# A routed-experts kernel: half rows and scatters for the late tiles, against whole rows and two tiles summed by 0/1 products

## The reference

```python
x = x + _L0_ffn_ref(_L0_cond_ref(x, cond_128, ...), L0_ffn_w_gate, L0_ffn_w_up, L0_ffn_w_down)
x = x + _L1_ffn_ref(_L1_cond_ref(x, cond_128, ...), L1_ffn_gate_w, L1_ffn_expert_w, L1_ffn_expert_b)

# _L1_ffn_ref: 32 experts, each token goes to its best two
logits = xf @ gate_w.T
w, idx = jax.lax.top_k(logits, 2)
w = jax.nn.softmax(w, axis=-1)
combine = zeros((T, 32)).at[arange(T)[:, None], idx].add(w)
out = sum over experts e of combine[:, e, None] * (xf @ expert_w[e].T + expert_b[e])
```

## Time and profile before

| | us |
|---|---|
| median of 3 runs | 294.91 |
| profiled execution | 294.77 |
| its span, first to last instruction | 292.9 |
| PE busy, share of the span | 261.6, 89% |
| DVE, ACT, POOL busy | 130.5, 77.4, 76.3 |
| bytes read from and written to HBM | 50.70 MB, 10.32 MB |

### The profile page before, as it was taken

How to read it: one execution, slowest core, us unless ns; L and a number is a source line. 1 busy time by engine, 2 the same in 40 slices (tenths; PEclk the granted TensorE clock), 3 DMA queues, 4 the chain that set the end, 5 groups by cost and what they waited for, 6 DMA issues and landing times.

```text
span 292.9 us, 4645 instructions
## 1 busy us (share of the span) xinstructions
PE 261.6 (89%) x1672; PEld 163.0 (56%) x1672; DVE 130.5 (45%) x386; ACT 77.4 (26%) x142; POOL 76.3 (26%) x77
## 2 busy tenths in 40 slices
PE   7877999999999999999999999999999999995000
PEld 3345677688777778788877764323333335662000
DVE  3368666767613335567313364105744112200374
ACT  2556665244011133333301112111011112121000
POOL 1522400000000000017150224576444542455000
PEclk9999999999999999999999999999999999999555
DMA  7990000000000100073049998259999999941896
GB/s 274 398 337 3 3 0 0 3 0 2 0 36 36 38 37 0 2 281 151 1 174 396 418 417 341 68 152 378 400 420 416 405 414 418 412 195 50 282 366 211
DMA packets 21671, 58.13 MB, mean 198 GB/s; under 512 B 4569, under 2 KB 12417, under 8 KB 17296
## 3 DMA queue, kind: packets, MB, share of 16 engines
q1 hardware_dynamic: 15216, 46.84, 41.2%
q0 software_dynamic: 3968, 8.43, 7.9%
q10 hardware_dynamic: 2464, 2.56, 2.5%
HBM read 50.70 MB, written 10.32 MB: 208 GB/s over the span
## 4 chain that ended last, share of the span: by engine, by line
PE 84%; DMA 7%; SPq 3%; DVE 2%; ACT 2%; issue 1%; ACTq 0%; POOLq 0%
PE bank L1338 27%; PE bank L1484 25%; PE bank L1520 14%; PE bank L1456 4%; DMA wbuf<-r_tab 4%; PE bank L1393 3%; DMA xp_first<-in_xp 2%; PE bank L1221 2%; PE bank L1414 2%; SPq L593 2%; PE bank L1400 1%; DMA r_tab<-res,row_halves 1%; PE bank L1283 1%; DVE y0lo L899 1%; PE bank L1231 1%
## 5 line engine op out<-in xcount | busy, mean ns | idle before, releaser
L1484 PE MATMUL bank<-wbuf,xT 128*32 128x512 f32 (+3 forms) x560 | 77.9, 512 | 0.0
L1520 PE MATMUL bank<-md,hid 128*128 128x512 f32 x176 | 48.2, 414 | 0.0
L623 POOL DMA_INDIRECT slots<-kept,sid x16 | 15.9, 994 | 122.1 <-DVE sid L1005 119.1
L1484 PEld LDWEIGHTS bank<-wbuf,xT 128*64 128x64 f32 (+1 forms) x560 | 27.9, 124 | 34.9 <-issue 27.6
L1520 PEld LDWEIGHTS bank<-md,hid 128*128 128x128 f32 x176 | 31.7, 189 | 8.3 <-issue 2.9
L1338 PE MATMUL bank<-y0hi,mg 128*128 128x512 f32 x88 | 35.2, 411 | 0.6 <-ACT y0hi L709 0.6
L1041 DVE COPY xT<-bank 128x512 f32<-128x512 f32 x21 | 14.5, 691 | 46.1 <-PE bank L1456 46.0
L827 ACT ACTIVATE res<-bank,recs 128x512 f32<-128x512 f32 (+1 forms) x27 | 16.0, 593 | 71.5 <-PE bank L1484 71.5
L1338 PE MATMUL bank<-y0hi,mu 128*128 128x512 f32 x88 | 33.7, 396 | 0.7 <-DVE mu L903 0.7
L1338 PE MATMUL bank<-y0lo,mg 128*128 128x512 f32 x88 | 33.7, 394 | 0.2 <-DVE y0lo L899 0.2
L1338 PE MATMUL bank<-y0lo,mu 128*128 128x512 f32 x88 | 33.6, 393 | 0.0
(11 more groups left out here) (187 smaller groups left out, 273.6 us busy)
## 6 DMA issues: line engine op xcount, KB each, us to landing
wbuf<-in_w SPq DMA_DIRECT2D x32, 1024.0 KB, 12.0
wbuf<-r_tab SPq DMA_DIRECT2D x8, 512.0 KB, 8.8
acc<-in_x SPq DMA_DIRECT2D x1, 2048.0 KB, 15.3
y_tab<-yv SPq DMA_DIRECT2D x8, 256.0 KB, 4.2
out<-acc ACTq DMA_DIRECT2D x8, 256.0 KB, 5.0
base<-in_base SPq DMA_DIRECT2D x3, 352.0 KB, 7.0
xp_first<-in_xp SPq DMA_DIRECT2D x1, 1040.0 KB, 6.9
xp_second<-in_xp SPq DMA_DIRECT2D x1, 1040.0 KB, 9.1
```

What stands on the lines that cost most here:

```text
L623: pool.indirect_dma_start(out=slots, out_offset=bass.IndirectOffsetOnAxis(ap=sid[:, j, k:k + 1], axis=0), in_=rec[:, j, k], in_offset=None ...
L1484: v = mm(in_place(RS[n % 2], h)[p0:p0 + w], xT[x_slot(t)][:, c, p0:p0 + w], wbuf[buffer(r)][:, c, columns(h)], start=(c == 0), stop=(c == ...
L1520: v = mm(DN[j % 2][:], hid[:, t, part, c], md[:, c], start=(c == 0 and part == 0), stop=(c == HC - 1 and part == 1))
```

## The change

- The steps in halves are gone. All 21 tiles are whole rows, with two places of `xT`. A scatter is 2 KB for each row.
- Only tiles 0 to 18 are scattered (TD = 19). The rows of tiles 19 and 20 stay in SBUF: ACT writes the scaled rows, rounded to float32r, to `rows{i}0`, and DVE computes the rest, scale times bank minus rounded, to `rows{i}1` (`low_part`). For each of the two tiles DVE builds a matrix `hot[i]` of 0 and 1, 128 rows by 1024 tokens (`one_hot`, from a new word 3 of the records). PE multiplies it with the rows for each block j of 128 tokens (`add_up`): two tiles, two parts, 8 blocks, 32 products of 128x512 in float32r.
- Rows of `r_tab` that no tile writes must be zero, so SP fills the table with zeros at the start, 4 MB, and POOL waits for that before its first scatter.
- The parts of `r_tab` are read as 8 DMAs of 512 KB with 4 KB pieces, after the scatters of tiles 0 to 18. DVE adds two rows for each block of 128 tokens (`add_part`) and then the block's bank of `add_up` (`add_hot`): 24 additions of 128x512 where there were 16.
- There is a 17th weight buffer, number 9, in the room of `stmp` and `htmp`; `combT`, the counters and lists moved to other room. Load 9 waits for the end of the hidden stage, ahead of the fifth store of y. Load 13 goes ahead of the last store of y. Loads 14 to 16 come after the records and a new wait: the gather of tile 5 must have landed. From 17 on a load waits for a product.
- DVE waits for the stores of y before it counts; `bodies` is read on DVE after the two `low_part`, and on PE between the last product and the first of `add_up`.

```diff
-NW = 2 * U
+NW = 2 * U + 1
-BESIDE_STORE = {4: (3, 4), 5: (5, 6, 9), 6: (7, 8, 10), 7: (11, 12)}
+BESIDE_STORE = {4: (3, 4, 9), 5: (5, 6, 10), 6: (7, 8, 11), 7: (12, 13)}
-STEPS = [(t, None) for t in range(FIRST_B)] + [(t, h) for h in range(2) for t in range(FIRST_B, TS - 1)] + ...
+HOT = 2
+TD = TS - HOT
...
 # SP
+            sp.dma_start(r_tab.rearrange("(p r) d -> p r d", p=P), a["zero"].unsqueeze(1).to_broadcast([P, 2 * NT, D])).then_inc(zero_in, 16)
...
+                if i == MIDDLE:
+                    sp.wait_ge(hhi_done, 2 * HC)
+                    sp.wait_ge(hlo_done, 2 * HC)
...
-            for r in range(13, NA):
+            sp.wait_ge(yg_in[FIRST % U], 16 * (FIRST // U + 1))
+            for r in range(14, NA):
                 load_w(r)
...
             for b in range(U):
-                static = len(range(b, TS, U))
+                static = len(range(b, TD, U))
                 sp.wait_ge(res_out[b], bodies * 16 + 16 * static if b < XU else 16 * static)
-            load_parts(0)
-            sp.wait_ge(right_out, 16 * (TS - FIRST_B))
-            load_parts(1)
+            for j in range(NT):
+                sp.dma_start(part(j), r_tab_v[:, 2 * j:2 * j + 2]).then_inc(part_in[j], 16)
...
 # POOL
+            pool.wait_ge(zero_in, 16)
+            for t in range(2):
+                scatter_tile(t)
...
-            for n in range(TS - LAG, NS):
-                scatter_step(n)
+            for t in range(TS - LAG, TD):
+                scatter_tile(t)
...
 # DVE
+            def low_part(i):
+                t = TD + i
+                dve.wait_ge(res_done, t + 1)
+                nc.vector.scalar_tensor_tensor(hot_rows(i, 1), RS[t % 2][:], recs[:, t, 2:3].bitcast(F32), hot_rows(i, 0).bitcast(F32),
+                                               ALU.mult, ALU.subtract).then_inc(low_rows, 1)
...
+            def add_part(j):
+                dve.wait_ge(part_in[j], 16)
+                for k in range(2):
+                    link(nc.vector.tensor_tensor(acc[:, j], acc[:, j], part(j)[:, k], ALU.add))
+            def add_hot(j):
+                dve.wait_ge(hot_mm, j + 1)
+                nc.vector.tensor_tensor(acc[:, j], acc[:, j], hot_bank(j)[:], ALU.add).then_inc(sum_done, 1)
+            for j in range(NT):
+                add_part(j)
+                if j >= TPH:
+                    add_hot(2 * (j - TPH))
+                    add_hot(2 * (j - TPH) + 1)
...
 # PE
+            def add_up(i, j):
+                for half in range(2):
+                    v = mm(hot_bank(j)[:], hot[i][:].rearrange("p h l -> p (h l)")[:, P * j:P * (j + 1)], hot_rows(i, half),
+                           start=(i == 0 and half == 0), stop=(i == HOT - 1 and half == 1))
+            pe.wait_ge(hot_done, HOT)
+            pe.wait_ge(low_rows, 1)
+            for j in range(6):
+                add_up(0, j)
+            pe.wait_ge(low_rows, HOT)
+            pe.wait_ge(res_done, bodies * XU + TS)
+            for j in range(6):
+                add_up(1, j)
+            for j in range(6, NT):
+                add_up(0, j)
+                add_up(1, j)
```

More of the change, by code:

```diff
@@ L162, in down_steps @@
 def down_steps(b):
-    end = (b - MIDDLE + 1) * DC * D * 4
+    end = (b - BY_DOWNS + 1) * DC * D * 4
     tile = 2 * HC * P * 4
@@ L171, in released @@
     return last_use(b) + 1
+LAST_USE = {buffer(r): max(t for t in range(TS) if any(g[2] == r for g in TILES[t])) for r in LOADS}
+DEAD = sorted((b for b in range(NA) if b >= XU), key=lambda b: (LAST_USE[b], b))
+HOT_AT, PART_AT, ROWS_AT = DEAD[0], DEAD[1:1 + NT // 2], DEAD[1 + NT // 2]
+assert max(LAST_USE[b] for b in (*PART_AT, ROWS_AT)) < TD - 1
 C_ID = 0
@@ L462, in x_slot, with height, part, hot_rows @@
         def x_slot(t):
[L464 to L480, removed]
+            return t % 2
+        def height(t):
+            return sum(w for _, w, _, _ in TILES[t])
+        def part(j):
+            return wbuf[PART_AT[j // 2]][:, 2 * (j % 2):2 * (j % 2) + 2]
+        def hot_rows(i, half):
+            return rows_split[i][half][:]
+        def hot_bank(j):
+            return bank[(4 + j) % 8]
         def recs_group(t):
@@ L823, in _, with evac @@
             weight_tanh(NT - 1)
[L825 removed]
+            def evac(n, b, slot, bank_, rows_=P):
                 act.wait_ge(r_mm, n + 1)
[L827 to L830 removed]
+                out = hot_rows(slot - TD, 0) if TD <= slot < TS else res[b][0:rows_]
+                nc.scalar.activation(out, bank_[0:rows_], ACT.Copy, scale=recs[0:rows_, slot, 2:3].bitcast(F32)).then_inc(res_done, 1)
+            for t in range(TS):
+                if t == 2:
                     combt_evac(1)
@@ L1483, in product @@
                     for p0, w, r, _ in TILES[t]:
-                        v = mm(in_place(RS[n % 2], h)[p0:p0 + w], xT[x_slot(t)][:, c, p0:p0 + w], wbuf[buffer(r)][:, c, columns(h)], start=(c == 0), stop=(c == DC - 1))
+                        v = mm(RS[t % 2][p0:p0 + w], xT[x_slot(t)][:, c, p0:p0 + w], wbuf[buffer(r)][:, c], start=(c == 0), stop=(c == DC - 1))
                 if c1 == DC:
@@ L1598, in _ @@
                 transposes(t)
-                product(t - 1, 0, DC, 0 if t > FIRST_B else None)
-            for t, h in STEPS[STEP[TS - 2, 0] + 1:]:
-                product(t, 0, DC, h)
+                product(t - 1, 0, DC)
+            product(TS - 1, 0, DC)
             pe.wait_ge(todo_done, 1)
```

148 lines of the change are left out of this document (67 added, 81 removed).

## The result

The median is 290.71 us (4 runs, 290.29 to 290.76) against 294.75 us for the kernel before (4 runs, 294.3 to 295.05): a ratio of 0.9848, 95% interval 0.9812 to 0.9884. By the medians that is 4.0 us less, where 3.2 us had been forecast. The profiled execution took 290.29 us with a span of 288.5, so the span is 4.4 us shorter, and nothing changed in what lies around it.

What follows compares the result with a forecast made beforehand. PE bounds to 267.6 us, then a 25.3 us tail of scatter, 4 MB read, additions and store. Additions from 269.9 plus 17.2, then 2.6, give span 289.7; plus 1.87 and 0.14, 291.7 us; range 290.4 to 294.2.

Steps and rivals of the forecast that it cites:

- the mechanism: Tail after PE: table read starts 5.9 us earlier, DVE gives back 3 with 24 additions, fed without waits; 3.2 us faster.
- the register read and the branch: On DVE between the second low_part and the first addition: 0.8 us, additions starting at 269.9 us.
- Scatter and read: Tile 18's scatter issued at 261.34, landed at 264.5; table read starts 264.8, first part 268.5, last by 283.0 us.
- Rival 1: Tile 18's scatter lands late in full queues, 6.7 us instead of 3.2: 293.8 us; chance 0.14.
- Rival 3: Uncovered read and branch on DVE cost a 6.7 us code fetch, additions from 276.6: 298.4 us, slower; chance 0.08.
- The additions: DVE's tail: 16 from SBUF at 0.73 us and 8 from PSUM at 0.69, 17.2 us, ending at 287.1.
- The forecast's low end: Range's lower end, 290.4 us: no cost for the register read (-0.8) and PSUM additions overlapped (-0.5).
- The tail end: From the last addition's end to the span's end, one 256 KB store: 2.6 us, unchanged.
- The hidden work: 0/1 matrices, 7.7 us of PE products, about 12 us of zero fill, 17th buffer and added wait cost nothing.
- rival 2: Added wait for tile 5's gather delays load 17 past its slack by about 1.3 us, reaching PE: 293.0 us; chance 0.08.

Runs made afterwards that it cites:

- the last version: Changed kernel with todo read ahead of low_part, additions interleaved, and the second row of parts 0 to 3 added on PE: 297.12 us, ratio 0.9832.

## Why the mechanism came out right and two steps of the sum wrong

**The mechanism held.** The read of the table starts early, DVE takes over as the bound, and it is fed by both the parts and PE. The run with four more additions (tail +2.9 us) and the one with eight fewer (-3.4 us) show this from both sides.

**Two steps failed.** The prediction put the register read and the branch wholly behind the second `low_part`, 0.8 us in series; they began together with it, and only 0.39 us stood out. And it priced 24 additions at 17.2 us; they took 16.5, since seven of them start 0.60 us after their predecessor. Both errors went the same way and make 1.1 of the 1.2 us by which the span came out shorter than the 289.7 forecast.

**PE.** Predicted end of the tiles 267.45, measured 267.45, with no gap from 180 us on.

**Scatter and read.** The scatter was put at 261.34, and is at 261.27. It lands 2.6 us later, not 3.2 (as the free queues of the earlier trace rows, not the half row), and the read starts at 264.01, 0.8 us earlier than said. The first part is there 3.6 us later, at 267.6; the last one, issued at 267.3, takes 10.5 us: 277.8, so 1.46 us apart. None of that reaches the end, since DVE is ready only after 269.03. Rival 1 did not occur; it would have needed 6.7 us.

**The register read and the branch.** The term I had called the least known was taken as 0.8 us and is 269.42 - 269.03 = 0.39 us. Its length was about right; the overlap was missed. Line L1208 in the trace (`x1: shortest/median/longest` in ns, start in us):

```profile
L1208 DVEq TENSOR_LOAD <-todo x1: 544/544/544, 268.3 to 268.3; - x1
L1208 DVEq FUSED_REGOPS  x1: 213/213/213, 268.9 to 268.9; - x1
```

The load takes 0.54 us and the register work behind it 0.21, together the 0.75 of the forecast. But DVE's sequencer starts the load at 268.3, while DVE itself runs the second `low_part` (268.28 to 269.03). From the load to the first addition it is 1.1 us, of which 0.7 lie beside `low_part`. The branch is 0.07 us in the chain (L1209). The prediction says that no row shows such a read on DVE. The trace of the kernel before does have one, at the old place, and beside the copy that starts at 253.50:

```profile
L1198 DVEq TENSOR_LOAD <-todo x1: 550/550/550, 253.5 to 253.5; - x1
```

So both the length and the overlap could have been read before. The Trainium skill (DMA: Bandwidth & Descriptors, Latency and other measured facts) puts the floor of such a load at about 600 ns; this trace, with 544 ns, comes near it, and what the sum lacked is the overlap. Rival 3 priced a fetch of code at 6.7 us; none is seen, for this short jump.

**The additions.** Taken as 16 x 0.73 + 8 x 0.69 = 17.2 us, measured 285.91 - 269.42 = 16.5 us. This is the other mis-sized term. The sum took 0.73 us for the 16 from SBUF and 0.69, the duration and a gap, for the 8 from PSUM. But an addition that does not wait for the one before it starts 0.60 us after it, before the other's 0.69 us are over: the two of L1223 take 1.28 us together, and the next of L1218 starts at 277.88, 1.20 us after 276.68, for two. Of the 23 distances in the chain seven are of this kind, 16 are 0.72 to 0.73. The groups by shape, which answer, could not show it, because an instruction's duration hardly changes:

```profile
L1218 DVE TENSOR_TENSOR acc<-acc,wbuf 128x512 f32<-128x512 f32 x16 | 11.1, 691 | 0.8 <-issue 0.4
L1223 DVE TENSOR_TENSOR acc<-acc,bank 128x512 f32<-128x512 f32 x8 | 5.1, 684 | 0.1
```

The forecast's low end had allowed 0.5 us for this, and the true size is 0.7. The reordered additions confirm the cause: the same count, without the dependence between neighbours, 0.60 us from start to start where no part is waited for.

**The tail end.** 288.5 - 285.91 = 2.6 us, as said. Together: 289.7 - 0.4 - 0.7 = 288.6, and the span is 288.5; the last 0.1 is `low_part`, which ends at 269.03 and not 269.12. The medians hide 0.2 us of this: that of the changed kernel is 0.42 us above its profiled execution, where 0.14 had been added, and that of the kernel before came out at 294.75, not 294.91.

**The hidden work.** The 0/1 matrices take 0.18 + 1.22 us between copies of turned tiles. The 32 products take 7.55 us beside the additions, as computed, at a granted clock of 1.00. The zero fill is issued at 11.4 us and takes 25.1 us to land, twice the 12 us of the forecast; two of the first loads, of x and of `slots`, are under way until 22 and 24 us, and that it shares the queues with them is the likely reason. It is over at 36.5 us, and the first scatter comes more than 100 us later. The gather of tile 5 lands at 190.4 + 4.0 = 194.4 us, and SP's loads 14 to 16 go out from 195.15, as before at 195.23, so rival 2 did not occur; the run without the wait agrees. The first load of the next burst, now number 17, lands at

```profile
L544 SPq DMA_DIRECT2D wbuf<-in_w x1: 361/361/361, 204.0 to 204.0; - x1
...
DMA to landing us min/median/max: 11.6/11.6/11.6
```

204.0 + 11.6 = 215.6 us, 2.4 us earlier than in the earlier trace rows, where I had said about 3. It is slack only: with 16 buffers the time is the same.

**Left open.** What DVE and ACT wait for at 194 to 203 us on the slower chips. It is there with and without the added wait and with 16 buffers, and while it lasts the DMA queues are full (367 GB/s from 199.5 to 204.1 us), but so they are on the first chip (384). Whether the kernel before has it too, no trace shows; that it is slower by the same 7 us speaks for it. Where the 3.1 and 2.5 us went that two profiled executions lost before 77 us was not followed up.

## What to carry to other kernels

When a transfer is taken off the path, count at once what the engine behind it has to do: here the first part came 6.8 us earlier (267.6 against 274.36), the first addition 4.9 and the end 4.4, so the next gain was fewer DVE additions, not a faster read. Price a chain of vector instructions by the distance between starts, separately for those that wait for the one before and those that don't, and never by mean duration alone. Look in the old trace for every instruction that the change moves, in the rows of the sequencers too: the register read was there, with its length and its overlap. Before an engine's work is reordered, lay its steps against the landing time of each input: in the last version the wait for three parts used up what four additions less had won.

## What the runs showed of the hardware that was not expected

- A DVE addition of 128x512 float32 that waits for its predecessor's semaphore starts 0.72 to 0.73 us after it, one that doesn't 0.60 us. Both show a duration of 0.69 us. The Trainium skill (VectorE: DVE Perf Modes, The DRAIN you can't avoid) reports that eight copies take the same time with a semaphore after each as with one after the last. The Trainium skill (VectorE: DVE Perf Modes, Rules for kernel authors) advises to minimize the count of operations, not of semaphores. Here 24 additions took 1.4 us less by order alone, waits for parts included, so a wait on the semaphore had a price.
- A register load on DVE (544 ns at L1208) started together with the DVE instruction ahead of it in the list, and cost only what stuck out behind that instruction.
- Reading 4 MB of a table back: 512 KB every 1.46 us in 4 KB pieces, 1.54 us with stores beside it, 1.66 us in 1 KB pieces (with one of SP's issues at 2.31 us among them).
- One kernel differed by 7 us between chips (294.8 and 301.9 us for the kernel before), with 4.4 to 5.6 us of it in one place where PE waited, in every trace taken there.
